# A mixture-of-experts stage whose expert weights are loaded from DRAM for each tile, with all tile rows loaded beforehand

## The chip, the core and the metric

The kernel runs on one core of one Trainium2 chip. The metric is the device time of one execution in microseconds (us). The core has five engines that run side by side and wait for each other with semaphores: TensorE (PE in the profile, with its weight loads as PEld), VectorE (DVE), ScalarE (ACT), GpSimd (POOL) and SyncE (SP). SP computes nothing here: it waits on semaphores and issues DMAs. Each engine works through its own program in order.

## The reference

Two layers are computed over 2048 tokens of 128 features. The last part of the second layer is a mixture of experts (MoE) with top-1 routing: each token goes through one of 8 experts, each a small two-layer network with its own weights.

```
hn = layernorm(xn) * ln2_g + ln2_b          # 2048 x 128
e  = argmax(hn @ gate_w + gate_b)           # one of 8 experts for each token
y  = relu(hn @ w1[e] + b1[e]) @ w2[e] + b2[e]     # w1: 128x512, w2: 512x128, all float32
x  = x + y                                  # (and the residuals of the other parts)
```

Everything before this (a recurrent filter and a gated network, attention, two Mamba scans) is outside the change.

## The kernel before

The program is a row of stages with a barrier of all engines between them (`end_stage`, line 59). The MoE is the last pair of stages.

`moe_prep_stage` (from line 1325) normalises the tokens, computes the gate, picks the expert and sorts the tokens by expert: each expert's tokens fill whole tiles of 128 rows, so there are at most NSLOT = 16 + 8 - 1 = 23 tiles. `S.eid` holds the expert of each tile, `S.pos` the row that each token goes to. The rows are scattered to DRAM (`S.x_dram`) by 16 indirect DMAs on POOL (line 1392), after a DMA on SP has filled `S.x_dram` with zeros (line 1372). In the same stage SP loads the weights of all 8 experts into one SBUF tensor `S.wall`: w1 as one DMA (line 1365), b1 (line 1366), b2 copied to all 128 partitions (line 1367) and w2 in eight DMAs (line 1369). SP waits for them at its end (line 1375).

`moe_stage` (from line 1486) runs over the 23 tiles, software-pipelined by hand. For tile s:

- SP: `load(s)` (line 1516) waits until tile s-3 is through (`y_psum`) and loads the 128 rows, 64 KB, into one of three buffers `x`; then `store(s-2)` (line 1522) waits for the result of tile s-2 and stores it to `S.y_dram`. The two alternate, so load(s+1) is queued behind store(s-2).
- DVE: reads the tile's expert number from `S.eid` into a register (line 1574) and copies that expert's 1156 columns of `S.wall` into one of three buffers `cur` (line 1577).
- PE: in its round s it transposes the rows of tile s+1 (line 1589, waits for the load), multiplies tile s by w1 in 4 matmuls that the profile shows as 8 records (line 1611), and then does the second layer of tile s-1: b2 through a matmul with a row of ones (line 1594, 2 records) and w2 (line 1597, 8 records).
- ACT: scales the transposed rows (line 1548), relu with bias b1 in four pieces (line 1565), copies the result out of PSUM into one of two buffers `y` (line 1555); before that copy it waits until the buffer's last store has landed (line 1554).

When all 23 stores have landed, POOL gathers the rows back to token order with 16 indirect DMAs (line 1539), DVE adds them to the residual (line 1581), and SP writes the output (line 1653).

Of the kernel before, what the change touches and what calls it, by code (L numbers as in the profile page):

```python
# [12 lines left out]
F32 = mybir.dt.float32  # L13
# [4 lines left out]
ACT = mybir.ActivationFunctionType  # L18
AX = mybir.AxisListType

P = 128
# [11 lines left out]
NE, NF = 8, 512  # L33
NFB = NF // P
NSLOT = NT + NE - 1
W2_AT = NF + NFB
B2_AT = W2_AT + NF
WROW = B2_AT + P
DI, NS, KC, DR = 256, 16, 4, 8
NB = DI // P  # L40

# [1281 lines left out]
def moe_prep_stage(nc, S, dr):  # L1323
# [4 lines left out]
    with ExitStack() as ctx:  # L1328
# [3 lines left out]
        def sem(n):  # L1332
            return S.enter_sem(nc, f"xp_{n}")
# [16 lines left out]
        w_load, dve_c, act_c, pool_c = sem("w_load"), sem("dve_chain"), sem("act_chain"), sem("pool_chain")  # L1350
        var_ready, rstd_ready, xn_ready, xn_psum, hn_ready = sem("var"), sem("rstd"), sem("xn_r"), sem("xn_psum"), sem("hn_r")
        lg_psum, oh_ready, counts = sem("lg_psum"), sem("oh_r"), sem("counts")
        all_in = sem("all_in")
        zeros_ready, zeroed, pos_ready, scattered = sem("zeros_r"), sem("zeroed"), sem("pos_r"), sem("scattered")
        block = ctx.enter_context(nc.Block())
        NCONST = 7
# [4 lines left out]
        @block.sync  # L1361
        def _(sp):
            sp.dma_start(gw[:, :], dr["gate_w"]).then_inc(w_load, 16)
            sp.dma_start(gb[:, :], dr["gate_b"]).then_inc(w_load, 16)
            sp.dma_start(S.wall[:, :, 0:NF], dr["w1"].rearrange("e h f -> h e f")).then_inc(all_in, 16)
            sp.dma_start(S.wall[:, :, NF:W2_AT], dr["b1"].rearrange("e p b -> p e b")).then_inc(all_in, 16)
            sp.dma_start(S.wall[:, :, B2_AT:WROW], dr["b2"].unsqueeze(0).to_broadcast([P, NE, P])).then_inc(all_in, 16)
            for e in range(NE):
                sp.dma_start(S.wall[:, e, W2_AT:B2_AT].rearrange("p (b h) -> p b h", h=P),
                             dr["w2"][e].rearrange("(b p) h -> p b h", p=P)).then_inc(all_in, 16)  # L1370
            sp.wait_ge(zeros_ready, 1)
            sp.dma_start(S.x_dram.rearrange("(s p) d -> p s d", p=P),
                         zeros[:, :].unsqueeze(1).to_broadcast([P, NSLOT, P])).then_inc(zeroed, 16)
            sp.wait_ge(w_load, 32)
            sp.wait_ge(all_in, 16 * (3 + NE))

        @block.gpsimd
        def _(pool):
# [107 lines left out]
def moe_stage(nc, S, dr):  # L1486

    with ExitStack() as ctx:  # L1488
        def sb(n, shape, dt=F32):
            return ctx.enter_context(nc.sbuf_tensor(f"xe_{n}", shape, dt))  # L1490

        def sem(n):
            return S.enter_sem(nc, f"xe_{n}")

        W = 3
        cur = sb("cur", [P, W, WROW])
        x, xT = sb("x", [P, W, P]), sb("xT", [P, 2, P])
        mid, y = sb("mid", [P, 2, NFB, P]), sb("y", [P, 2, P])
        ones = sb("ones", [1, P])
        picked = sem("picked")  # L1500
        moved = sb("moved", [P, NT, P])
        t_bank, m_bank, y_bank = S.banks[0:2], S.banks[2:4], S.banks[4:6]
        loaded = [sem(f"loaded{w}") for w in range(W)]
        stored = [sem("stored0"), sem("stored1")]
        gathered = [sem(f"gathered{c}") for c in range(NCH)]
        turned, xT_ready, mid_psum, mid_ready, y_psum, y_ready = (sem("turned"), sem("xT_r"), sem("mid_psum"), sem("mid_r"),
                                                                  sem("y_psum"), sem("y_r"))
# [6 lines left out]
        @block.sync  # L1514
        def _(sp):
            def load(s):
                w = s % W
                if s >= W:
                    sp.wait_ge(y_psum, s - W + 1)
                sp.dma_start(x[:, w, :], S.x_dram[P * s:P * (s + 1), :]).then_inc(loaded[w], 16)  # L1520

            def store(s):
                sp.wait_ge(y_ready, s + 1)
                sp.dma_start(S.y_dram[P * s:P * (s + 1), :], y[:, s % 2, :]).then_inc(stored[s % 2], 16)  # L1524

            for s in range(NSLOT):
                load(s)
                if s >= 2:
                    store(s - 2)
            store(NSLOT - 2)  # L1530
            store(NSLOT - 1)

        @block.gpsimd
        def _(pool):
            pool.memset(ones[:, :], 1.0).then_inc(ones_ready, 1)
            pool.wait_ge(stored[0], 16 * ((NSLOT + 1) // 2))
            pool.wait_ge(stored[1], 16 * (NSLOT // 2))
            for i in range(NT):
                pool.indirect_dma_start(moved[:, i, :], None, S.y_dram,  # L1539
                                        bass.IndirectOffsetOnAxis(ap=S.pos[:, i:i + 1], axis=0)).then_inc(gathered[i // TPC], 16)  # L1540

        @block.scalar
        def _(act):
            def turn(s):
                act.wait_ge(turned, s + 1)
                if s >= 2:
                    act.wait_ge(mid_psum, s - 1)
                act.activation(xT[:, s % 2, :], t_bank[s % 2][:, 0:P], ACT.Identity, bias=V("ln2_b"),  # L1548
                               scale=V("ln2_g")).then_inc(xT_ready, 1)

            def out(s):
                act.wait_ge(y_psum, s + 1)
                if s >= 2:
                    act.wait_ge(stored[s % 2], 16 * (s // 2))
                act.activation(y[:, s % 2, :], y_bank[s % 2][:, 0:P], ACT.Copy).then_inc(y_ready, 1)  # L1555

            turn(0)
            for s in range(NSLOT):
                if s + 1 < NSLOT:
                    turn(s + 1)  # L1560
                act.wait_ge(mid_psum, s + 1)
                if s >= 2:
                    act.wait_ge(y_psum, s - 1)
                for f in range(NFB):
                    act.activation(mid[:, s % 2, f, :], m_bank[s % 2][:, P * f:P * (f + 1)], ACT.Relu,
                                   bias=cur[:, s % W, NF + f:NF + f + 1]).then_inc(mid_ready, 1)
                if s >= 1:
                    out(s - 1)
            out(NSLOT - 1)

        @block.vector
        def _(dve):
            for s in range(NSLOT):
                e = dve.value_load(S.eid[0:1, s:s + 1], min_val=0, max_val=NE - 1)
                if s >= W:
                    dve.wait_ge(y_psum, s - W + 1)
                dve.tensor_copy(cur[:, s % W, :].unsqueeze(1), S.wall[:, bass.ds(e, 1), :]).then_inc(picked, 1)  # L1577
            for c in range(NCH):
                dve.wait_ge(gathered[c], 16 * TPC)
                r = S.res[:, TPC * c:TPC * (c + 1), :]  # L1580
                dve.tensor_tensor(r, r, moved[:, TPC * c:TPC * (c + 1), :], ALU.add).then_inc(added, 1)  # L1581

        @block.tensor
        def _(pe):
            def turn(s):
                pe.wait_ge(loaded[s % W], 16 * (s // W + 1))
                if s >= 2:
                    pe.wait_ge(xT_ready, s - 1)
                pe.transpose(t_bank[s % 2][:, 0:P], x[:, s % W, :], S.ident[:, :]).then_inc(turned, 1)  # L1589

            def output(s):
                if s >= 2:
                    pe.wait_ge(y_ready, s - 1)
                pe.matmul(y_bank[s % 2][:, 0:P], ones[:, :], cur[0:1, s % W, B2_AT:WROW], start=True, stop=False)  # L1594
                for f in range(NFB):
                    pe.wait_ge(mid_ready, NFB * s + f + 1)
                    mm = pe.matmul(y_bank[s % 2][:, 0:P], mid[:, s % 2, f, :], cur[:, s % W, W2_AT + P * f:W2_AT + P * (f + 1)],  # L1597
                                   start=False, stop=(f == NFB - 1))
                mm.then_inc(y_psum, 1)

            pe.wait_ge(ones_ready, 1)
            turn(0)
            for s in range(NSLOT):
                if s + 1 < NSLOT:
                    turn(s + 1)
                pe.wait_ge(xT_ready, s + 1)
                if s >= 2:
                    pe.wait_ge(mid_ready, NFB * (s - 1))
                pe.wait_ge(picked, s + 1)
                for f in range(NFB):  # L1610
                    mm = pe.matmul(m_bank[s % 2][:, P * f:P * (f + 1)], cur[:, s % W, P * f:P * (f + 1)], xT[:, s % 2, :],  # L1611
                                   start=True, stop=True)
                mm.then_inc(mid_psum, 1)
                if s >= 1:
                    output(s - 1)
            output(NSLOT - 1)


def moe(nc, S, dr):
    with ExitStack() as ctx:  # L1620
        S.pos = ctx.enter_context(nc.sbuf_tensor("x_pos", [P, NT], U32))
        S.eid = ctx.enter_context(nc.sbuf_tensor("x_eid", [P, NSLOT], I32))
        S.wall = ctx.enter_context(nc.sbuf_tensor("x_wall", [P, NE, WROW], F32))
        S.x_dram, S.y_dram = (nc.dram_tensor(f"x_{n}", [NSLOT * P, P], F32).ap() for n in ("rows", "done"))
        moe_prep_stage(nc, S, dr)
        S.end_stage(nc)
        moe_stage(nc, S, dr)
        S.end_stage(nc)
# [82 lines left out]
```

## Time and profile before

| | us |
|---|---|
| median of 3 runs | 1839.95 (1839.89 to 1840.34) |
| the profiled execution | 1845.69 |
| its span, first to last instruction | 1844.0 |
| MoE stage until its last result is in SBUF | 1646.79 to 1813.93 |
| gather, residual and output after it | 1813.95 to 1844.0 |

| engine | busy us of the span | share |
|---|---|---|
| PE | 1148.8 | 62% |
| DVE | 1260.3 | 68% |
| ACT | 845.7 | 46% |
| POOL | 508.4 | 28% |

The busy shares are means over stages with different limits; the stages before 1595 us are bound by other engines than the MoE stage is. For a change in one stage, the views to read are those of that stage: who waits for whom, the chain of work that ended last, and the timeline in order of time. A time of an instruction that begins with L is its line in the code; SPq and DVEq are the sequencers of SP and DVE, which issue DMAs and work on registers, and are not counted as busy. PEclk is the granted TensorE clock as a share of full speed: 0.50 is 1.2 GHz, 1.00 is 2.4 GHz.

### The profile page before, as it was taken

Reading aid. Unit: us, or ns where it says so; the run is one execution under the profiler, and the core shown is the slowest. Engines: PE = TensorE matmul, PEld = TensorE weight load, DVE = VectorE, ACT = ScalarE, POOL = GpSimd, SP = SyncE. Lnnn points to the kernel's source line nnn. Section 1 sums busy time; section 2 is a strip of 40 time slices with the busy share of each in tenths; the row PEclk is TensorE's granted clock in tenths of the full one; section 3 lists DMA queues with packets and bytes.
Section 4 is the critical chain, followed back from the end, with each engine's and each line's share of the span. In section 5 each row is a group of like instructions: output and inputs, shape, how many; then the busy total and the mean of one; then the engine's idle time right before and its main releaser. Section 6 shows DMA issues by size and latency. Waiting matters only on the chain. (4 is left out here: it accounts for less than half of the span.)

```text
span 1844.0 us, 17746 instructions
## 1 busy us (share of the span) xinstructions
PE 1148.8 (62%) x5865; PEld 398.3 (22%) x5865; DVE 1260.3 (68%) x1893; ACT 845.7 (46%) x1217; POOL 508.4 (28%) x473
## 2 busy tenths in 40 slices
PE   0341499999999999999873133337513333526662
PEld 0130022222222222222330000004200000425552
DVE  8943899999999999996111599991139999410000
ACT  2220067777777777777625244431524444202220
POOL 1201000000000000000002699980249999130003
PEclk9765599999999999999986555557855555655555
DMA  0012010001001100000003666600176552310001
GB/s 28 0 62 83 24 58 1 1 22 46 10 1 38 39 1 1 1 2 1 3 19 119 125 127 137 137 1 22 63 171 138 124 108 43 110 59 18 17 18 53
DMA packets 64682, 93.51 MB, mean 51 GB/s; under 512 B 8998, under 2 KB 29750, under 8 KB 64590
## 3 DMA queue, kind: packets, MB, share of 16 engines
q1 hardware_dynamic: 63566, 90.27, 19.8%
q0 software_dynamic: 1024, 2.10, 0.4%
q8 instruction: 47, 0.77, 0.2%
q14 instruction: 45, 0.37, 0.1%
HBM read 74.88 MB, written 17.17 MB: 50 GB/s over the span
## 5 line engine op out<-in xcount | busy, mean ns | idle before, releaser
L658 DVE TENSOR_REDUCE at_mpart<-psum 128x1 f32<-128x512 f32 x1024 | 656.5, 685 | 49.3 <-PE psum L719 30.0
L637 ACT ACTIVATE at_probs<-psum 128x1024 f32<-128x1024 f32 x512 | 496.2, 1021 | 272.8 <-PE psum L748 272.6
L761 PE MATMUL psum<-at_probs,at_vg 128*32 128x512 f32 x2048 | 273.6, 606 | 0.4 <-ACT at_probs L637 0.4
L748 PE MATMUL psum<-at_qs,at_ks 75*128 75x512 bf16 x1024 | 269.3, 384 | 1.3 <-ACT at_probs L637 0.2
L719 PE MATMUL psum<-at_ks,at_qs 64*128 64x512 bf16 x512 | 207.9, 406 | 84.9 <-DMA at_km<-k_parts 50.6
L723 PE MATMUL psum<-at_km,at_qm 64*128 64x512 bf16 x512 | 207.9, 406 | 0.0
L613 POOL CAST at_m<-at_mneg 128x16 bf16<-128x16 f32 x16 | 3.1, 197 | 698.2 <-DVE at_mneg L663 698.2
L1225 POOL TENSOR_TENSOR msf_inject<-msf_dus,msf_bs 128x512 f32<-128x512 f32 x128 | 159.7, 1299 | 28.5 <-DMA msf_cs<-m_bc 28.5
L1225 POOL TENSOR_TENSOR msb_inject<-msb_dus,msb_bs 128x512 f32<-128x512 f32 x128 | 158.4, 1265 | 27.0 <-DMA msb_cs<-m_bc 27.0
L1244 PE MATMUL psum<-msf_hc,m_stack 128*32 128x512 f32 x256 | 61.0, 1042 | 161.6 <-DVE msf_hc L1169 152.6
L1244 PE MATMUL psum<-msb_hc,m_stack 128*32 128x512 f32 x256 | 60.1, 1027 | 160.9 <-DVE msb_hc L1169 151.9
L719 PEld LDWEIGHTS psum<-at_ks,at_qs 64*128 64x128 bf16 x512 | 47.7, 93 | 385.0 <-DVE at_mpart L658 331.1
L1577 DVE COPY xe_cur<-x_wall 128x1156 f32 x23 | 17.5, 763 | 159.0 <-PE psum L1597 134.4
L1153 ACT ACTIVATE psum<-msf_dts,m_aneg 128x512 f32<-128x512 f32 x128 | 85.5, 686 | 48.6 <-DVE msf_hp L1196 19.4
L748 PEld LDWEIGHTS psum<-at_qs,at_ks 75*128 75x128 bf16 x1024 | 78.2, 98 | 135.3 <-issue 52.0
L1153 ACT ACTIVATE psum<-msb_dts,m_aneg 128x512 f32<-128x512 f32 x128 | 85.5, 686 | 47.1 <-DVE msb_hp L1196 19.2
L1196 DVE TENSOR_TENSOR_SCAN psum<-psum,msb_last,msb_inject 128x512 f32<-128x512 f32 x66 | 82.5, 1273 | 0.0
L1196 DVE TENSOR_TENSOR_SCAN psum<-psum,msf_last,msf_inject 128x512 f32<-128x512 f32 x66 | 82.5, 1273 | 0.0
L1539 POOL DMA_INDIRECT xe_moved<-x_done,x_pos x16 | 15.7, 981 | 173.3 <-DMA x_done<-xe_y 168.7
L1589 PE MATMUL psum<-ident,xe_x 128*128 128x128 f32 x23 | 10.8, 472 | 83.4 <-DMA xe_x<-x_rows 83.4
L1239 PE MATMUL psum<-m_u,m_diag 128*32 128x512 f32 x128 | 30.3, 1028 | 49.5 <-PEq L62 49.5
L1169 DVE TENSOR_TENSOR msf_hc<-psum,msf_cs 128x512 f32<-128x512 f32 x88 | 58.6, 667 | 0.0
(273 smaller groups left out, 1421.3 us busy)
## 6 DMA issues: line engine op xcount, KB each, us to landing
msf_dts<-m_dt SPq DMA_DIRECT2D x32, 256.0 KB
msf_dus<-m_dtu SPq DMA_DIRECT2D x32, 256.0 KB
msb_dts<-m_dt SPq DMA_DIRECT2D x32, 256.0 KB
msb_dus<-m_dtu SPq DMA_DIRECT2D x32, 256.0 KB
at_qs<-q_parts SPq DMA_DIRECT2D x48, 96.0 KB
at_ks<-k_parts SPq DMA_DIRECT2D x48, 96.0 KB
msf_bs<-m_bc SPq DMA_DIRECT2D x16, 256.0 KB
msf_cs<-m_bc SPq DMA_DIRECT2D x16, 256.0 KB
```

What stands on the lines that cost most here:

```text
L637: act.activation(probs[:, u % 2, p, :], s_pair[p], ACT.Exp, scale=float(HD) ** -0.5).then_inc(probs_ready, 1)
L658: dve.reduce_max(mpart[:, s % 2, 2 * jp + b, i, kc:kc + 1], ring[x % 3], AX.X).then_inc(ring_free, 1)
L719: pe.matmul(ring[x % 3], S.qs[0:HALF, buf, q], S.ks[0:HALF, buf, k], start=True, stop=True)\
L723: pe.matmul(ring[y % 3], S.qm[64:64 + HALF, buf, q], S.km[64:64 + HALF, buf, k], start=True, stop=True)\
L748: mm = pe.matmul(s_banks[p][b], S.ks[0:DM, g % 2, j * T + kt * P:j * T + (kt + 1) * P], S.qs[0:DM, g % 2, j * T + c * CH:j * T + (c + 1) * ...
L761: mm = pe.matmul(o_bank[VW * j:VW * (j + 1), :], vg[:, g % 2, kt, j, :], probs[:, u % 2, j // 2, CH * (j % 2):CH * (j % 2 + 1)], start=(kt ...
L1153: act.activation(decay[k % ND], dts[:, i % 2, j, :], ACT.Exp, scale=S.aneg[:, n:n + 1]).then_inc(decay_ready, 1)
L1169: dve.tensor_tensor(hc[:, r % 2, j, :], hv[by_dve[k] % NH2], cs[:, c % 2, q, :], ALU.mult).then_inc(dve_weighed, 1)
L1196: dve.tensor_tensor_scan(h, decay[k % ND], inject[:, k % NI, :], before if c else 0.0, ALU.mult, ALU.add).then_inc(scanned, 1)
L1225: pool.tensor_tensor(inject[:, k % NI, :], dus[:, i % 2, j, :], bs[:, c % 2, q, :], ALU.mult).then_inc(injected, 1)
L1239: pe.matmul(y_bank[i % 2][GC * j:GC * (j + 1), :], S.diag[:, b, GC * j:GC * (j + 1)], S.u[:, b, cols(c)], start=True, stop=False, tile_pos ...
L1244: mm = pe.matmul(y_bank[i % 2][GC * j:GC * (j + 1), :], S.stack[:, :], hc[:, r % 2, j, :], start=False, stop=(q == NQ - 1), tile_position= ...
```

## The change

`S.wall` is gone, with its eleven loads in the prep stage and the wait for them. In the MoE stage DVE no longer reads expert numbers or copies weights. SP does both: `load(s)` reads the expert number of tile s into a register of SP and issues four DMAs from DRAM at an address that depends on it (w1 256 KB, b1 2 KB, w2 256 KB, b2 0.5 KB), into one of five buffers. The rows of all 23 tiles are loaded by four DMAs at the start of the stage (`rows(n)`, six tiles each), the first ahead of load(0), the others behind it. Results have a buffer for each of the 23 tiles, so ACT's wait for a store's landing is gone. store(s-5) stands behind load(s) on SP.

```diff
-            sp.dma_start(S.wall[:, :, 0:NF], dr["w1"].rearrange("e h f -> h e f")).then_inc(all_in, 16)
-            sp.dma_start(S.wall[:, :, NF:W2_AT], dr["b1"].rearrange("e p b -> p e b")).then_inc(all_in, 16)
-            sp.dma_start(S.wall[:, :, B2_AT:WROW], dr["b2"].unsqueeze(0).to_broadcast([P, NE, P])).then_inc(all_in, 16)
-            for e in range(NE):
-                sp.dma_start(S.wall[:, e, W2_AT:B2_AT].rearrange("p (b h) -> p b h", h=P),
-                             dr["w2"][e].rearrange("(b p) h -> p b h", p=P)).then_inc(all_in, 16)
...
-            sp.wait_ge(all_in, 16 * (3 + NE))
...
-        W = 3
+        W = 5
+        NX = 4
+        XT = -(-NSLOT // NX)
...
                 if s >= W:
                     sp.wait_ge(y_psum, s - W + 1)
-                sp.dma_start(x[:, w, :], S.x_dram[P * s:P * (s + 1), :]).then_inc(loaded[w], 16)
+                e = sp.value_load(S.eid[0:1, s:s + 1], min_val=0, max_val=NE - 1)
+                sp.dma_start(w1[:, w, :], dr["w1"][bass.ds(e, 1)].rearrange("o h f -> h (o f)")).then_inc(loaded[w], 16)
+                sp.dma_start(b1[:, w, :], dr["b1"][bass.ds(e, 1)].rearrange("o p b -> p (o b)")).then_inc(loaded[w], 16)
+                sp.dma_start(w2[:, w, :, :], dr["w2"][bass.ds(e, 1)].rearrange("o (b p) h -> p (o b) h", p=P))\
+                    .then_inc(loaded[w], 16)
+                sp.dma_start(b2[:, w, :], dr["b2"][bass.ds(e, 1)]).then_inc(loaded[w], 16)
 
             def store(s):
                 sp.wait_ge(y_ready, s + 1)
-                sp.dma_start(S.y_dram[P * s:P * (s + 1), :], y[:, s % 2, :]).then_inc(stored[s % 2], 16)
-
-            for s in range(NSLOT):
+                sp.dma_start(S.y_dram[P * s:P * (s + 1), :], y[:, s, :]).then_inc(stored, 16)
+
+            def rows(n):
+                part = slice(XT * n, min(XT * (n + 1), NSLOT))
+                sp.dma_start(x[:, part, :], S.x_dram.rearrange("(s p) d -> p s d", p=P)[:, part, :]).then_inc(x_in[n], 16)
+
+            rows(0)
+            load(0)
+            for n in range(1, NX):
+                rows(n)
+            for s in range(1, NSLOT):
                 load(s)
-                if s >= 2:
-                    store(s - 2)
-            store(NSLOT - 2)
-            store(NSLOT - 1)
+                if s >= W:
+                    store(s - W)
+            for s in range(NSLOT - W, NSLOT):
+                store(s)
...
-                if s >= 2:
-                    act.wait_ge(stored[s % 2], 16 * (s // 2))
-                act.activation(y[:, s % 2, :], y_bank[s % 2][:, 0:P], ACT.Copy).then_inc(y_ready, 1)
+                act.activation(y[:, s, :], y_bank[s % 2][:, 0:P], ACT.Copy).then_inc(y_ready, 1)
...
-            for s in range(NSLOT):
-                e = dve.value_load(S.eid[0:1, s:s + 1], min_val=0, max_val=NE - 1)
-                if s >= W:
-                    dve.wait_ge(y_psum, s - W + 1)
-                dve.tensor_copy(cur[:, s % W, :].unsqueeze(1), S.wall[:, bass.ds(e, 1), :]).then_inc(picked, 1)
...
-                pe.wait_ge(loaded[s % W], 16 * (s // W + 1))
+                pe.wait_ge(x_in[s // XT], 16)
...
-                pe.wait_ge(picked, s + 1)
+                pe.wait_ge(loaded[s % W], 16 * 4 * (s // W + 1))
```

## Rows read from the trace of the kernel before

**Rows 1.** Chain of work that ended last, one tile: start, us, what
```profile
1723.52 0.32 SPq L1524
1723.89 1.88 DMA xe_x<-x_rows
1725.81 0.48 PE psum L1589
1726.29 1.71 PE psum L1611 x8
1727.99 0.72 PE psum L1594 x2
1728.71 2.02 PE psum L1597 x8
1730.75 0.29 ACT xe_y L1555
```

**Rows 2.** Waits, 1646 to 1815 us: who waited for whom, total us, times, longest
```profile
PE psum L1589 <- DMA xe_x<-x_rows: 83.4, 21, 30.3
```

**Rows 3.** Timeline of PE at the stage's end: start, us, line, count [idle before]
```profile
1801.54 0.48 PE L1589 MATMUL psum<-ident,xe_x 128*128 128x128 f32 x1 [2.69 <-DMA xe_x<-x_rows]
1801.81 1.92 PE L1611 MATMUL psum<-xe_xT,xe_cur 128*128 128x128 f32 x8
1803.65 0.79 PE L1594 MATMUL psum<-xe_cur,xe_ones 1*128 1x128 f32 x2
1804.38 2.08 PE L1597 MATMUL psum<-xe_cur,xe_mid 128*128 128x128 f32 x8
1806.24 1.92 PE L1611 MATMUL psum<-xe_xT,xe_cur 128*128 128x128 f32 x8
```

**Rows 4.** Timeline, first result of the stage on PE
```profile
1653.58 0.48 PE L1594 MATMUL psum<-xe_cur,xe_ones 1*128 1x128 f32 x2
1654.00 1.16 PE L1597 MATMUL psum<-xe_cur,xe_mid 128*128 128x128 f32 x8
```

**Rows 5.** Stretches: from:to, length, busy us (count) of PE, PEld, DVE, ACT, POOL, PEclk, DMA share, GB/s
```profile
1524.00:1529.00 5.00, 3.64 (x16) 0.68 (x16) 5.00 (x7) 3.19 (x6) 5.00 (x5) 0.50 1.07 211
1554.00:1555.00 1.00, 0.08 (x4) 0.00 (x0) 1.00 (x3) 0.52 (x1) 1.00 (x2) 0.85 0.00 0
1592.00:1595.00 3.00, 1.72 (x5) 0.41 (x3) 2.63 (x13) 0.00 (x0) 0.00 (x0) 1.00 0.00 0
1656.00:1658.00 2.00, 0.27 (x2) 0.28 (x2) 0.06 (x1) 0.00 (x0) 0.00 (x0) 0.67 0.23 66
1806.20:1813.60 7.40, 7.40 (x30) 6.22 (x28) 0.00 (x0) 1.70 (x6) 0.00 (x0) 0.50 0.06 18
```

**Rows 6.** DVE's sequencer, reading an expert number (ns min/median/max)
```profile
L1574 DVEq TENSOR_LOAD <-x_eid x23: 298/300/556, 1646.8 to 1791.5; - x23
L1574 DVEq FUSED_REGOPS  x23: 190/190/213, 1647.4 to 1791.8; - x23
L1577 DVEq FUSED_REGOPS  x23: 57/57/65, 1647.7 to 1798.9; - x23
```

**Rows 7.** Timeline of SP: DMA issues, start, us in all, count
```profile
1.24 2.07 SPq L135 DMA_DIRECT2D l_x<-in_x  x4
1596.21 0.43 SPq L1365 DMA_DIRECT2D x_wall<-in_w  x1
1601.59 8.27 SPq L1369 DMA_DIRECT2D x_wall<-in_w  x8
```

**Rows 8.** Timeline of the prep stage: what the scatter's first DMA waited for
```profile
1623.08 1.20 POOL L1392 DMA_INDIRECT x_rows<-xp_xn,x_pos  x1 [26.57 <-DVE x_pos L1459]
```

**Rows 9.** Timeline: last copy of a result, before the gather
```profile
1813.65 0.28 ACT L1555 ACTIVATE xe_y<-psum 128x128 f32<-128x128 f32 x1 [2.45 <-PE psum L1597]
```

**Rows 10.** Timeline of PE in the Mamba stage, second of two equal stretches
```profile
1550.44 1.94 PE L1244 MATMUL psum<-msb_hc,m_stack 128*32 128x512 f32 x8 [4.57 <-DVE msb_hc L1169]
1552.12 1.96 PE L1239 MATMUL psum<-m_u,m_diag 128*32 128x512 f32 x8
```

More of the change, by code:

```diff
@@ L35 @@
 NSLOT = NT + NE - 1
-W2_AT = NF + NFB
-B2_AT = W2_AT + NF
-WROW = B2_AT + P
 DI, NS, KC, DR = 256, 16, 4, 8
@@ L1352, in moe_prep_stage @@
         lg_psum, oh_ready, counts = sem("lg_psum"), sem("oh_r"), sem("counts")
-        all_in = sem("all_in")
         zeros_ready, zeroed, pos_ready, scattered = sem("zeros_r"), sem("zeroed"), sem("pos_r"), sem("scattered")
@@ L1493, in sem @@
             return S.enter_sem(nc, f"xe_{n}")
-        W = 3
-        cur = sb("cur", [P, W, WROW])
-        x, xT = sb("x", [P, W, P]), sb("xT", [P, 2, P])
-        mid, y = sb("mid", [P, 2, NFB, P]), sb("y", [P, 2, P])
+        W = 5
+        NX = 4
+        XT = -(-NSLOT // NX)
+        w1, w2, b1, b2 = sb("w1", [P, W, NF]), sb("w2", [P, W, NFB, P]), sb("b1", [P, W, NFB]), sb("b2", [1, W, P])
+        x, xT = sb("x", [P, NSLOT, P]), sb("xT", [P, 2, P])
+        mid, y = sb("mid", [P, 2, NFB, P]), sb("y", [P, NSLOT, P])
         ones = sb("ones", [1, P])
-        picked = sem("picked")
         moved = sb("moved", [P, NT, P])
@@ L1503, in moe_stage @@
         loaded = [sem(f"loaded{w}") for w in range(W)]
-        stored = [sem("stored0"), sem("stored1")]
+        x_in = [sem(f"x_in{n}") for n in range(NX)]
+        stored = sem("stored")
         gathered = [sem(f"gathered{c}") for c in range(NCH)]
@@ L1535, in _ @@
             pool.memset(ones[:, :], 1.0).then_inc(ones_ready, 1)
-            pool.wait_ge(stored[0], 16 * ((NSLOT + 1) // 2))
-            pool.wait_ge(stored[1], 16 * (NSLOT // 2))
+            pool.wait_ge(stored, 16 * NSLOT)
             for i in range(NT):
@@ L1565, in _ @@
                     act.activation(mid[:, s % 2, f, :], m_bank[s % 2][:, P * f:P * (f + 1)], ACT.Relu,
-                                   bias=cur[:, s % W, NF + f:NF + f + 1]).then_inc(mid_ready, 1)
+                                   bias=b1[:, s % W, f:f + 1]).then_inc(mid_ready, 1)
                 if s >= 1:
@@ L1585, in turn @@
             def turn(s):
-                pe.wait_ge(loaded[s % W], 16 * (s // W + 1))
+                pe.wait_ge(x_in[s // XT], 16)
                 if s >= 2:
                     pe.wait_ge(xT_ready, s - 1)
-                pe.transpose(t_bank[s % 2][:, 0:P], x[:, s % W, :], S.ident[:, :]).then_inc(turned, 1)
+                pe.transpose(t_bank[s % 2][:, 0:P], x[:, s, :], S.ident[:, :]).then_inc(turned, 1)
             def output(s):
@@ L1593, in output @@
                     pe.wait_ge(y_ready, s - 1)
-                pe.matmul(y_bank[s % 2][:, 0:P], ones[:, :], cur[0:1, s % W, B2_AT:WROW], start=True, stop=False)
+                pe.matmul(y_bank[s % 2][:, 0:P], ones[:, :], b2[:, s % W, :], start=True, stop=False)
                 for f in range(NFB):
                     pe.wait_ge(mid_ready, NFB * s + f + 1)
-                    mm = pe.matmul(y_bank[s % 2][:, 0:P], mid[:, s % 2, f, :], cur[:, s % W, W2_AT + P * f:W2_AT + P * (f + 1)],
+                    mm = pe.matmul(y_bank[s % 2][:, 0:P], mid[:, s % 2, f, :], w2[:, s % W, f, :],
                                    start=False, stop=(f == NFB - 1))
@@ L1608, in _ @@
                     pe.wait_ge(mid_ready, NFB * (s - 1))
-                pe.wait_ge(picked, s + 1)
+                pe.wait_ge(loaded[s % W], 16 * 4 * (s // W + 1))
                 for f in range(NFB):
-                    mm = pe.matmul(m_bank[s % 2][:, P * f:P * (f + 1)], cur[:, s % W, P * f:P * (f + 1)], xT[:, s % 2, :],
+                    mm = pe.matmul(m_bank[s % 2][:, P * f:P * (f + 1)], w1[:, s % W, P * f:P * (f + 1)], xT[:, s % 2, :],
                                    start=True, stop=True)
@@ L1622, in moe @@
         S.eid = ctx.enter_context(nc.sbuf_tensor("x_eid", [P, NSLOT], I32))
-        S.wall = ctx.enter_context(nc.sbuf_tensor("x_wall", [P, NE, WROW], F32))
         S.x_dram, S.y_dram = (nc.dram_tensor(f"x_{n}", [NSLOT * P, P], F32).ap() for n in ("rows", "done"))
```

## The prediction

> **What bounds the kernel now.** Only the MoE stage changes in its rhythm, so the page's shares of the whole span say little; I read the stage's own views. First the chain that ended last. One tile takes 7.52 us in it: SP issues a store (0.32), then the load of the rows takes 1.88 from issue to landing, then PE works 0.48 + 1.71 + 0.72 + 2.02 = 4.93, then ACT copies the result (0.29) and SP can issue the next store [rows 1]. The reader is to see that a DMA stands in the chain of each tile, although three buffers exist: the load of tile s+1 is queued on SP behind store(s-2), which waits for ACT's copy. The list of waits says the same: PE waited 83.4 us in 21 waits for rows, 30.3 of them from before the stage [rows 2], so about 53 us, 2.6 for each of 20 tiles. Then the timeline of the last tiles, where all rows are in: PE goes from line 1589 at 1801.54 to the next line 1611 at 1806.24 without a wait for rows, 4.70 us [rows 3]. That is what PE needs for a tile at 1.2 GHz. Last the clock: it is 0.50 nearly throughout, but the first result was computed at the higher level, with line 1597 in 1.16 us where it takes 2.02 later [rows 1, 4].
>
> **What is removed from the chain.** The row load (1.88), the copy (0.29), the store's issue (0.32) and the gaps between them leave the chain: 7.52 - 4.70 = 2.82 us per tile. The rows come beforehand, and nothing on PE waits for SP's stores. What is next is one of three: PE at 1.2 GHz (4.70), PE at 2.4 GHz, or SP, which now issues five DMAs per tile instead of two.
>
> **PE at 2.4 GHz.** Line 1594 takes 0.42 until line 1597 starts (1654.00 - 1653.58) [rows 4]; line 1597 until the next group 1806.24 - 1804.38 = 1.86 at 1.2 GHz [rows 3], of which 8 records of 128 float32 columns stream half as long at the double clock; 1.16 with its end [rows 4], so 1.0 until the next can start. Line 1611 likewise 1803.65 - 1801.81 = 1.84 becomes 0.99, the transpose 0.27 becomes 0.11. Sum 2.5 us.
>
> **SP per tile.** The trace has no read of an expert number on SP, but DVE makes the same one: 0.298 for the load, 0.190 for register operations, and with its check and gaps 0.59 [rows 6]. Each of the four DMAs has an address from the register; the nearest row is DVE's 0.057 for its dynamic copy [rows 6], with a gap some 0.11, four times 0.43. Upper end: the 0.190 kind each time, with its gap 0.24, 0.96 in all. The issues: w1 0.43 as line 1365; w2 is the pattern of layer 0's input (128 partitions, four pieces of 512 B), 2.07 / 4 = 0.52; b1 and b2 not over 0.43 each [rows 7]. With gaps of 0.05: 0.59 + 0.43 + 0.43 + 0.52 + 0.86 + 0.20 = 3.03 us for a load; with the store's 0.32 + 0.05 [rows 1] 3.40. Bounds: 2.9 if the small ones and the address work cost less, 4.0 with the upper price of addresses. The w2 loads in the prep stage were issued every 8.27 / 8 = 1.03 us [rows 7], twice 0.52: there SP was held up by full queues, 256 KB each 1.03 us being 254 GB/s. A tile here moves 516 KB in and 64 KB out; at that rate 2.3 us, under the 3.40 of the issues, so the transfers hide behind the issuing and no queue stays full except at the start.
>
> The Trainium skill ("DMA: Bandwidth & Descriptors", Latency and other measured facts) gives a floor of some 600 ns for a tensor load. The trace differs, 0.298 here [rows 6], and decides; by the page's figure each tile would cost SP 0.3 us more, by an estimate 23 x 0.3 = 7 us on the total.
>
> **The clock.** Which of the two levels PE gets decides between 4.70 and SP's 3.40. What rows show: at the stage's start PE did line 1611 twice with a transpose between, from 1649.88 on without idle time, and at 1653.6 it ran at 2.4 GHz [rows 4]; it fell back after the first wait for rows, 1655.2 to 1657.7 [rows 5]. In the last 7.4 us of the stage PE was also without a long gap and stayed at 0.50 [rows 5]. There each stretch of full matmuls between two of line 1594 was 1.86 + 1.84 = 3.7 us. In Mamba, stretches of 3.6 us, eight records of line 1244 and eight of line 1239, come several times: the one from 1524.4 left the clock at 0.50, the equal one from 1550.4 raised it [rows 5, 10]. So stretches of this length raise it sometimes. After the change the stretch is w2, transpose, w1: 1.86 + 0.27 + 1.84 = 4.0 us, longer than all of these, and it comes each tile. I expect a rise within the first few tiles in which PE runs without waiting. Does it stay? At SP's pace PE idles 3.40 - 2.5 = 0.9 us per tile in small pieces; from 1592 to 1595 PE was busy for 1.72 of 3.0 us and the clock stayed at 1.00 [rows 5], and the fall in this stage came with 2.5 us idle in one piece. If it falls, PE lags, has no waits again, and rises again. I take 2.4 GHz for most of the stage.
>
> The skill ("TensorE: Matmul & The Clock Gate", Loop structure matters more than you think) says that matmuls back to back, with the DMAs overlapped, keep the clock up, and that a wait on a DMA before each matmul group lets it fall. The last 7.4 us, back to back and at 0.50 [rows 5], do not bear that out fully, which is why the slow clock keeps a chance below.
>
> **The other edits.** In prep the loads leave SP, not the path: the scatter waited for DVE's positions until 1623.08 [rows 8], with the zero fill long issued; the stage's SP wait ended before that. I cost this at nothing (bounds -1 and +0.5, should the DMA traffic have held up anything). DVE's copies (0.76 each) were beside PE; ACT's wait for a landed store did not end last. ACT per tile is about 1.9 us at either clock, under 3.40. The end, the last store and the gather, is the same.
>
> **The sum**, from the stage's start. Before, the last copy ended at 1813.93 [rows 9], 167.1 us after 1646.79. After: rows(0) 0.6, load(0) 3.0, the other three row DMAs 1.7; 2 MB are then asked for by 5.3 us and take about 8 us at 254 GB/s, which holds SP up by 1: 6.3. Loads 1 to 4: 4 x 3.03 = 12.1, to 18.4. Loads 5 to 22 with a store each: 18 x 3.40 - 0.37 = 60.8, to 79.2. The last lands some 1.7 later (rows land 1.88 from issue [rows 1]), 80.9; then w1 0.99, second layers of tiles 21 and 22 with 1.4 and 1.6, and ACT 0.3: 85.2. The gain is 167.1 - 85.2 = 82 us. Against the profiled execution 1845.69 becomes 1764 (its span 1762); it lies 5.7 above the median of the runs, all of it outside what changes, so the median goes from 1839.95 to 1758.
>
> **Rivals.** *The clock stays at 1.2 GHz* and PE is the bound: tile 1 can start at 11 us (load 1 issued by 9.3), its w1 and the layer before it take 4.5, then 21 x 4.70 = 98.7 and 2.8 for the end: 117. Gain 50, time 1790. For it: the rows of the last 7.4 us. Against it: the longer stretch. *SP's address work is dear* or the clock is up only in part: SP at 4.0 to 4.7 per tile adds 22 x 0.6 to 22 x 1.2, 13 to 27 us: 1771 to 1785. *Slower than before:* SP is the bound with an issue price for a DMA at a register's address that no row shows. From 167 - 15 = 152 us over 22 loads, 6.9 us per tile, it loses: that is 0.9 more for each of the four DMAs, three times the price of an issue. At 7.5 it would be 1853. Against it: every DMA of SP is already made by the same hardware queue at run time. *That it does nothing* needs PE to wait as before; since the rows no longer hang on results, only a clock and an SP both bad could do it.
>
> **How the numbers follow.** 0.61 for SP-bound at the high clock, 1747 to 1771, forecast 1758; 0.17 for 1771 to 1786; 0.17 for the slow clock, 1786 to 1796; 0.03 for SP between 5 and 6.9 us per tile; 0.02 for slower. The low end is SP at 2.9: 22 x 0.5 = 11 less. The range 1747 to 1792 leaves out about 0.15. What a measurement of this kernel can tell from no change is about 0.2%: faster 0.97, same 0.01, slower 0.02.
>
> **What would show it.** In the changed kernel's timeline SP issues without waits from load 1 on, a new one each 3.4 us with the five DMAs; PE's waits are for w1 or w2, some 0.9 us a tile; PEclk is near 1.00 from the third tile or so; line 1597 is near 1.16. I am wrong if PEclk stays 0.50 with PE without idle time (1790), if a dynamic issue is far over 0.5 us, or if PE waits on ACT at the high clock.

## The result, and the profile after

The changed kernel takes 1754.57 us in the median (1753.94 to 1760.18, 4 runs), beside 1839.92 for the kernel before (1835.68 to 1840.34, 4 runs). The ratio is 0.955, with an interval of 0.952 to 0.957: 85 us less. The profiled execution took 1753.94, its span 1752.0.

| | before | after |
|---|---|---|
| prep stage, first DMA issue | 1595.33 | 1586.34 |
| MoE stage begins | 1646.79 | 1637.82 |
| MoE stage until its last result is copied | 167.1 | 84.7 |
| from there to the end of the span | 30.0 | 29.5 |

Two things stand in this table. The stage lost 82.5 us. And it began 9.0 us earlier, all of which had been gained before the prep stage began, in stages whose code is the same. The stage begins between 1637 and 1647 us in all the kernels below, and not in the order of what they change. So differences between kernels are read from the stage's own length below, and the total only where it was taken in several runs.

SP in the changed kernel, one tile from its timeline (start, us, line):

```profile
1666.30 0.34 SPq L1512 DMA_DIRECT2D xe_w<-in_w  x1
1666.82 0.33 SPq L1513 DMA_DIRECT2D xe_b<-in_b  x1
1667.25 0.38 SPq L1514 DMA_DIRECT2D xe_w<-in_w  x1
1667.82 0.28 SPq L1516 DMA_DIRECT2D xe_b<-in_b  x1
1668.15 0.34 SPq L1520 DMA_DIRECT2D x_done<-xe_y  x1
1669.44 0.34 SPq L1512 DMA_DIRECT2D xe_w<-in_w  x1
```

Lines 1512 to 1516 are w1, b1, w2 and b2, line 1520 is a store of a result. From one w1 to the next it is 3.14 us, and nothing in between is a wait. The 0.95 us between the end of the store's issue at 1668.49 and the next w1 is the read of the expert number and the address. The instructions there, by line, with ns min/median/max:

```profile
L1511 SPq TENSOR_LOAD <-x_eid x23: 447/457/505, 1638.2 to 1711.5; - x23
L1511 SPq FUSED_REGOPS  x23: 152/152/187, 1638.8 to 1712.0; - x23
L1512 SPq FUSED_REGOPS  x23: 42/42/48, 1639.1 to 1712.2; - x23
L1512 SPq MOVE xe_w<-in_w x23: 29/29/43, 1639.2 to 1712.3; - x23
```

PE in the changed kernel, in its timeline where the clock rises:

```profile
1658.27 0.42 PE L1585 MATMUL psum<-ident,xe_x 128*128 128x128 f32 x1
1658.49 1.92 PE L1607 MATMUL psum<-xe_xT,xe_w 128*128 128x128 f32 x8
1660.33 0.78 PE L1590 MATMUL psum<-xe_b,xe_ones 1*128 1x128 f32 x2
1661.04 1.16 PE L1593 MATMUL psum<-xe_w,xe_mid 128*128 128x128 f32 x8
1662.03 0.27 PE L1585 MATMUL psum<-ident,xe_x 128*128 128x128 f32 x1
1662.14 1.06 PE L1607 MATMUL psum<-xe_xT,xe_w 128*128 128x128 f32 x8
```

Line 1585 is the transpose, 1607 is w1, 1590 the product of ones and b2, 1593 is w2. They answer to [rows 3 and 4]. w1 and w2 take 1.06 and 1.16 us where they took 1.92 and 2.08. The stretches of the changed kernel (length, busy us and count of PE, PEld, DVE, ACT, POOL, PEclk, DMA share, GB/s):

```profile
1637.80:1722.50 84.70, 70.02 (x437) 60.88 (x437) 0.00 (x0) 40.97 (x138) 0.19 (x1) 0.82 0.64 179
1656.00:1661.00 5.00, 5.00 (x21) 4.38 (x20) 0.00 (x0) 2.17 (x9) 0.00 (x0) 0.50 0.60 168
1661.00:1702.00 41.00, 37.68 (x275) 32.80 (x275) 0.00 (x0) 25.41 (x87) 0.00 (x0) 1.00 0.67 184
1702.00:1705.00 3.00, 0.34 (x4) 0.11 (x3) 0.00 (x0) 0.63 (x2) 0.00 (x0) 1.00 0.54 151
1705.00:1712.00 7.00, 6.98 (x29) 6.18 (x29) 0.00 (x0) 2.35 (x9) 0.00 (x0) 0.52 0.57 170
```

PEclk is 0.50 while the first loads arrive, 1.00 from 1661.0, and 0.50 again from about 1705 until 1712. What came before the fall is in the same trace. SP's timeline, then PE's, then the DMA queues from 1700 to 1703 us (packets, MB, share of the 16 engines' time):

```profile
1698.66 0.34 SPq L1512 DMA_DIRECT2D xe_w<-in_w  x1
...
1700.18 0.28 SPq L1516 DMA_DIRECT2D xe_b<-in_b  x1
...
1702.33 1.12 SPq L1513 DMA_DIRECT2D xe_b<-in_b  x1
...
1705.02 1.76 PE L1607 MATMUL psum<-xe_xT,xe_w 128*128 128x128 f32 x8 [2.68 <-DMA xe_b<-in_b]
...
q8 instruction: 1, 0.02, 3.9%
```

PE had nothing for 2.68 us, and the clock fell. Counted back from the last tile on both engines, the w1 product at 1705.02 is that of tile 18, and tile 18's loads are those issued from 1698.66 to 1700.46, on time and each at its usual length. Of the landings that the trace has for this tile's semaphore all but the last came by 1702.73, and the last at 1704.88. The issue on SP that took 1.12 us instead of 0.33 belongs to tile 19 and can't have held up tile 18. Both the late piece and the long issue overlap in time with one packet of 16 KB on q8, the queue that the profile names instruction: it took 1.87 us from 1701.20 (the 3.9% above). That this packet held them up is likely and not shown. The kernel before fell to the low level in its wait of 2.57 us [rows 5] too, but the size of one wait doesn't tell alone: in the kernel with rows per tile below, the clock fell at 1688.7 after waits of 1.09 and 1.49 us, and in the unbroken control it stayed up through one of 1.69.

PE's waits for weights are few and add up to 10.3 us, 5.0 of them for the first two tiles (the list of waits, the stage only):

```profile
PE psum L1607 <- DMA xe_b<-in_b: 10.3, 8, 2.8
```

against 83.4 for rows in the kernel before, 30.3 of them from before the stage [rows 2]. Once PE has caught up with the loads, from 1680 on, it waits for one now and then, 0.3 to 0.7 us, at the full clock, and SP waits once between two loads, for 0.3 us: that points to SP as the bound, which the experiments test.

### The profile page after: what moved, and what is told of

Same layout as the page of the kernel before. It is cut to its first block and busy times, and to the rows that moved or that the text cites. A ratio compares the mean times of both kernels' runs of the same rounds, so it can differ in the third digit from the quotient of the medians.

```text
span 1752.0 us, 17902 instructions
## 1 busy us (share of the span) xinstructions
PE 1101.0 (63%) x5865; PEld 358.7 (20%) x5865; DVE 1242.1 (71%) x1870; ACT 843.4 (48%) x1217; POOL 510.1 (29%) x473
## 5 line engine op out<-in xcount | busy, mean ns | idle before, releaser
L716 PE MATMUL psum<-at_ks,at_qs 64*128 64x512 bf16 x512 | 208.0, 406 | 85.2 <-DMA at_km<-k_parts 50.7
L1193 DVE TENSOR_TENSOR_SCAN psum<-psum,msf_last,msf_inject 128x512 f32<-128x512 f32 x66 | 82.5, 1274 | 0.0
L1193 DVE TENSOR_TENSOR_SCAN psum<-psum,msb_last,msb_inject 128x512 f32<-128x512 f32 x66 | 82.5, 1273 | 0.0
L1166 DVE TENSOR_TENSOR msb_hc<-psum,msb_cs 128x512 f32<-128x512 f32 x88 | 58.6, 667 | 0.0
L1139 ACT ACTIVATE msb_last<-psum 128x1 f32<-128x1 f32 x66 | 11.3, 171 | 88.8 <-DVE msb_hc L1166 88.8
```

Of the source, the lines that this page charges most:

```text
L716: pe.matmul(ring[x % 3], S.qs[0:HALF, buf, q], S.ks[0:HALF, buf, k], start=True, stop=True)\
L1166: dve.tensor_tensor(hc[:, r % 2, j, :], hv[by_dve[k] % NH2], cs[:, c % 2, q, :], ALU.mult).then_inc(dve_weighed, 1)
L1193: dve.tensor_tensor_scan(h, decay[k % ND], inject[:, k % NI, :], before if c else 0.0, ALU.mult, ALU.add).then_inc(scanned, 1)
```

## The experiments

All stage lengths are from the stage's first instruction to the copy of its last result, in the profiled execution of each kernel. The clock is the mean PEclk of the stage. A kernel for which no range of totals is given was executed once.

| kernel | stage us | clock in it | us per tile in steady state |
|---|---|---|---|
| before | 167.1 | 0.51 | 7.52 |
| changed | 84.7 | 0.82 | 2.50 to 3.8, one 7.28 |
| rows only, weights from SBUF | 66.7 | 0.90 | 2.50 |
| load ahead of the store | 62.5 | 0.95 | 2.50 |
| changed, fixed address | 70.4 | 0.88 | 2.50 |
| changed, half the bytes | 82.5 | 0.86 | 2.50 to 3.4, one 4.39 |
| changed, rows per tile | 93.7 | 0.80 | 2.50 to 5.8 |
| changed, three buffers | 117.3 | 0.64 | 3.2 to 6.3 |
| changed, broken stretch | 138.9 | 0.50 | 5.67 |
| changed, unbroken control | 84.8 | 0.88 | 2.73 to 4.7 |
| rows only, bias on DVE | 51.2 | 0.91 | 1.90 |
| load ahead of the store, bias on DVE | 48.8 | 0.94 | 1.90 |

**Rows only.** Is it the weights from DRAM, or the rows beforehand, that helped?

```diff
-                sp.dma_start(x[:, w, :], S.x_dram[P * s:P * (s + 1), :]).then_inc(loaded[w], 16)
...
+            for n in range(NX):
+                part = slice(XT * n, min(XT * (n + 1), NSLOT))
+                sp.dma_start(x[:, part, :], S.x_dram.rearrange("(s p) d -> p s d", p=P)[:, part, :]).then_inc(x_in[n], 16)
+            for s in range(NSLOT):
+                sp.wait_ge(y_ready, s + 1)
+                sp.dma_start(S.y_dram[P * s:P * (s + 1), :], y[:, s, :]).then_inc(stored, 16)
```

> One part of the change alone: the rows of all tiles are loaded beforehand and all results keep a buffer, as in the changed kernel, but the weights stay as before (eight experts in SBUF, DVE copies the tile's expert). Theory: the rhythm of the changed kernel is set by SP's issuing (3.15 us a tile in its trace), and the gain comes from rows that no longer wait for results; then without SP's work TensorE is the bound at its 2.5 us a tile, the clock rises after the first tiles, and the stage takes 62 to 67 us until its last copy, against 84.7 in the changed kernel: 1732 to 1738 in all. Rival 1, loading the weights from DRAM is what helped: then this kernel is slower than the changed one, at 1775 to 1790 (TensorE at 1.2 GHz, 4.65 us a tile, or DVE's copies in the way). Rival 2, TensorE and not SP bounds the changed kernel: then both are within 5 us.

Measured: stage 66.7 us, 1742.1 in all (1739.5 to 1745.9, 4 runs; ratio to the kernel before 0.950, 0.947 to 0.952). The total is some 4 us over the upper end of the expectation, the stage within it; this kernel's stage began at 1644.0, 6 us later than the changed kernel's. Its stretches:

```profile
1644.00:1710.70 66.70, 62.17 (x437) 55.85 (x437) 17.53 (x23) 40.86 (x138) 0.19 (x1) 0.90 0.16 45
1660.00:1700.00 40.00, 40.00 (x305) 36.14 (x305) 12.21 (x16) 28.32 (x96) 0.00 (x0) 1.00 0.10 27
```

PE is busy for 40.00 of 40.00 us at the full clock: it is the bound, at 2.50 us a tile. The weights from DRAM did not help; they cost the stage 84.7 - 66.7 = 18 us. All the gain is in the rows and results.

**Load ahead of the store.** Does it take all rows beforehand, or only another order on SP?

```diff
                 load(s)
-                if s >= 2:
-                    store(s - 2)
-            store(NSLOT - 2)
-            store(NSLOT - 1)
+                if s >= XW:
+                    store(s - XW)
+            for s in range(NSLOT - XW, NSLOT):
+                store(s)
```

(on the kernel before, with XW = 5 buffers for rows and for results instead of 3 and 2)

> The kernel before with nothing but a deeper row queue: five buffers for the rows and five for the results, the rows still loaded tile by tile, and store(s-5) instead of store(s-2) behind load(s); weights as before. Theory (the row load stood behind a store that waits for a result two tiles back, and that order alone cost the 2.8 us a tile and the clock): the same as the kernel with all rows loaded beforehand, stage 65 to 69 us, total about 1740. Rival (it takes all rows in SBUF beforehand, because a row load in the loop still lands late): 75 us or more.

Measured: stage 62.5 us, below the expectation; 1734.0 in all (1732.6 to 1736.1, 4 runs; ratio 0.943, 0.940 to 0.946). Every interval between results was 2.50 us from the first on, but for the last two (2.39 and 1.50), behind which no more tile comes. It is 4 us shorter than with all rows beforehand: the clock was up by 1648.0, 6.4 us after the stage's start, where the kernel with all rows beforehand had it 13.2 us after (1657.2). Half of the 4 us is that the first rows come sooner: PE's first instruction is 1.9 us after the stage's start here and 3.9 us there. The rest is the clock, which rose 4.5 us after PE's first instruction and not 9.3; why it did so is not shown. So five buffers and an order in which no load stands behind a late store are all that the stage needed.

**Fixed address.** What do reading the expert number and the address in a register cost? This kernel leaves out the routing: tile s takes the weights of expert s modulo 8.

```diff
-                e = sp.value_load(S.eid[0:1, s:s + 1], min_val=0, max_val=NE - 1)
+                e = s % NE
...
-                sp.dma_start(w1[:, w, :], dr["w1"][bass.ds(e, 1)].rearrange("o h f -> h (o f)")).then_inc(loaded[w], 16)
+                sp.dma_start(w1[:, w, :], dr["w1"][e:e + 1].rearrange("o h f -> h (o f)")).then_inc(loaded[w], 16)
```

> The changed kernel with the expert number of each tile a constant (tile number modulo 8), so that SP neither reads it nor works out addresses; the same bytes are moved, but the wrong experts' weights are applied, so the output is not the reference's. It measures the price of the register address. Theory (SP's issuing is the bound): 0.46 + 0.15 + 0.02 for the read and its check, 0.04 + 0.03 for each address, and their gaps leave SP, 3.15 becomes about 2.0 us a tile, TensorE's 2.5 binds, and the stage takes 68 to 75 us instead of 84.7. Rival (the DMA engines bound it, 0.67 of their time taken in the changed kernel at 184 GB/s): no change, 82 to 87 us.

Measured: 70.4 us, as the theory said, with as many bytes. The loads that waited for nothing followed each other every 1.73 us, where the changed kernel needs 2.80. The experts also come in another order than in the changed kernel. In the middle of the stage:

```profile
1660.00:1700.00 40.00, 40.00 (x306) 36.13 (x305) 0.00 (x0) 28.36 (x97) 0.00 (x0) 1.00 0.83 232
```

PE is the bound again, and the DMA engines carried 232 GB/s at a share of 0.83, against 184 at 0.67 in the changed kernel. The transfers were not what limited that kernel. They aren't far from it either.

**Half the bytes.** The same question from the other side: from the sixth tile on half of w1 and w2 is left out.

```diff
+                nf, nb = (NF, NFB) if s < W else (NF // 2, NFB // 2)
-                sp.dma_start(w1[:, w, :], dr["w1"][bass.ds(e, 1)].rearrange("o h f -> h (o f)")).then_inc(loaded[w], 16)
+                sp.dma_start(w1[:, w, 0:nf], dr["w1"][bass.ds(e, 1), :, 0:nf].rearrange("o h f -> h (o f)")).then_inc(loaded[w], 16)
```

> The changed kernel with w1 and w2 of every tile from the sixth on loaded only by half (256 of 512 columns, two of four blocks), the same number of DMAs; the other half of each buffer keeps what an earlier tile left there, so the output is not the reference's. Theory (SP's issuing): the stage stays at 83 to 86 us, DMA share falls from 0.67 to about 0.4. Rival (the transfers bound it): 18 tiles of half the bytes save up to 1 us each or more, 65 to 75 us. A small gain of 1 to 3 us would say that full queues hold SP up now and then (the three issues of about 1 us in the changed kernel's trace).

Measured: 82.5 us, 2.1 less than the changed kernel, just outside the theory's 83 to 86:

```profile
1641.20:1723.80 82.60, 67.87 (x437) 58.34 (x437) 0.00 (x0) 41.03 (x138) 0.20 (x1) 0.86 0.45 127
1665.00:1705.00 40.00, 37.70 (x275) 32.62 (x274) 0.00 (x0) 25.41 (x87) 0.00 (x0) 1.00 0.36 100
```

DMA share fell to 0.36, and PE was busy for 37.70 of 40 us, against 37.68 of 41 in the changed kernel. The 2 us are not SP's: it ended its last load 76.7 us after the stage's start, beside 76.4 in the changed kernel. They are PE's at the end, which began its last w1 1.4 us after that load and not 3.9, since in this execution the clock did not fall again. So half the bytes gave SP nothing, and an issue of 1.57 us instead of 0.38 occurred here too:

```profile
L1515 SPq DMA_DIRECT2D xe_w<-in_w x23: 383/383/1572, 1643.7 to 1717.1; - x23
```

**Rows per tile.** The rows part undone, the weights part kept.

```diff
                 sp.dma_start(b2[:, w, :], dr["b2"][bass.ds(e, 1)]).then_inc(loaded[w], 16)
+                sp.dma_start(x[:, w, :], S.x_dram[P * s:P * (s + 1), :]).then_inc(x_in[w], 16)
...
-            rows(0)
             load(0)
-            for n in range(1, NX):
-                rows(n)
```

> The changed kernel with one part undone: the rows of tile s are loaded in load(s), behind its weights, into five buffers, instead of beforehand. Theory (SP's issuing is the bound): each tile costs SP 0.43 + 0.05 more, 3.15 becomes 3.6 us, and the stage grows by 17 x 0.45 = 8 us less 2 for the shorter start: 88 to 94 us, if the clock stays up as long. Rival (the transfers or TensorE bound it): 82 to 86 us.

Measured: 93.7 us, 9.0 more, and SP's period grew from 3.14 to 3.62 us:

```profile
1671.15 0.35 SPq L1512 DMA_DIRECT2D xe_w<-in_w  x1
1671.68 0.34 SPq L1513 DMA_DIRECT2D xe_b<-in_b  x1
1672.12 0.38 SPq L1514 DMA_DIRECT2D xe_w<-in_w  x1
1672.69 0.28 SPq L1516 DMA_DIRECT2D xe_b<-in_b  x1
1673.02 0.34 SPq L1517 DMA_DIRECT2D xe_x<-x_rows  x1
1673.42 0.42 SPq L1521 DMA_DIRECT2D x_done<-xe_y  x1
1674.77 0.35 SPq L1512 DMA_DIRECT2D xe_w<-in_w  x1
```

One issue more per tile, some 0.48 us more per tile: SP sets the pace. Between these two executions the rows beforehand are worth 9 us, and 17 tiles by 0.48 account for 8 of them. The clock fell twice here and once in the changed kernel.

**Three buffers.**

```diff
-        W = 5
+        W = 3
```

> The changed kernel with three weight buffers instead of five (and store(s-3) behind load(s)). Load(s) may then start only when the second layer of tile s-3 is done. Theory: from there the issues take 2.8 and the landing 1.7 us, 4.5 to 4.9 in all, for which TensorE has only one tile's work, so it idles about 2.4 us in every two tiles; at 2.4 GHz a tile would take 3.7 us, and when the clock falls 4.7; stage 95 to 115 us. Rival (five buffers do nothing since SP is behind anyway): 83 to 88 us.

Measured: 117.3 us, 2 over the upper end of the theory; the rival is out. The clock was up for only 33 of the 117 us (mean 0.64), so the size that I had wrong was the share of the slow clock: with 13 waits of PE for loads, 16.9 us in all, and 4.65 us a tile at the low level, less is left of the gain.

**Broken stretch, and its control.** What raises the clock?

```diff
                 pe.wait_ge(loaded[s % W], 16 * 4 * (s // W + 1))
+                pe.matmul(S.banks[6][:, 0:P], ones[:, :], b2[:, s % W, :], start=True, stop=True)
```

> The changed kernel with one more product of the row of ones and b2 in each tile, into an unused part of PSUM, between the transpose and w1; the result isn't used. It breaks the stretch w2, transpose, w1 in two, as the last tiles of the kernel before had it broken, and costs TensorE 0.42 us at 2.4 GHz and 0.72 at 1.2. Theory (an unbroken stretch of full matmuls raises the clock): PEclk stays at 0.50 in nearly all of the stage, 5.4 us a tile, 125 to 135 us. Rival (TensorE at work without idle time is enough): it rises as before, 2.9 us a tile stay under SP's 3.15, and the stage takes 84 to 88 us.

The control has the same product at another place:

```diff
+                pe.matmul(S.banks[6][:, 0:P], ones[:, :], b2[:, s % W, :], start=True, stop=True)
                 pe.matmul(y_bank[s % 2][:, 0:P], ones[:, :], b2[:, s % W, :], start=True, stop=False)
```

> The control of the kernel with the broken stretch: the same extra product of ones and b2 in each tile, but directly ahead of the one that is there, so that w2, transpose and w1 still follow each other without it. Theory (the place matters, an unbroken stretch raises the clock): PEclk rises after some tiles as in the changed kernel, 2.7 to 2.9 us a tile stay under SP's 3.15, stage 84 to 92 us. Rival (the place doesn't matter, only that the extra product takes time from full matmuls): PEclk stays at 0.50 and the stage takes 135 to 140 us, as with the broken stretch (138.9).

Measured: 138.9 us with the stretch broken and 84.8 with the control. The stage of the first, then of the control:

```profile
1644.50:1783.50 139.00, 130.65 (x483) 107.33 (x483) 0.00 (x0) 41.72 (x138) 0.20 (x1) 0.50 0.39 109
```

```profile
1642.70:1727.50 84.80, 70.14 (x483) 61.60 (x483) 0.00 (x0) 40.96 (x138) 0.19 (x1) 0.88 0.65 179
```

PE did the same instructions in both (483 records). In the first it was busy 130.65 of 139 us, with no wait for loads after the start, and the clock never left 0.50. The place of one product, two records in each tile, decides 54 us. That the broken tile took 5.67 and not 5.4 us is part of the 138.9 being over the expected 135: from the transpose to the next product it was 0.35 us there, where it is 0.21 to w1 in the changed kernel at the same level, and w1 took 2.01 until the next start and not 1.84. The next kernels show the same from the other side.

**The bias on DVE.** On the kernel with rows only, DVE adds b2 while it copies the result out of PSUM; the product with ones and ACT's copy go.

```diff
+            def out(s):
+                dve.wait_ge(y_psum, s + 1)
+                dve.tensor_tensor(y[:, s, :], y_bank[s % 2][:, 0:P], cur[:, s % W, B2_AT:WROW], ALU.add).then_inc(y_ready, 1)
...
-                pe.matmul(y_bank[s % 2][:, 0:P], ones[:, :], cur[0:1, s % W, B2_AT:WROW], start=True, stop=False)
```

> The kernel with only the rows loaded beforehand (weights from SBUF), with b2 added by DVE while it copies the result out of PSUM, in place of the product of ones and b2 on TensorE and of ACT's copy. Theory (TensorE's 2.5 us bounds that kernel, 0.42 of it for the product): 2.1 us a tile, and at the start the clock rises no later; stage 66.7 - 21 x 0.42 = 57 to 59 us, total 8 to 10 under that kernel. Rival (ACT at 1.6 us with its waits, or DVE with 0.76 for the weights and 0.3 for the result, becomes the bound): 2.3 us a tile or more, 62 us and up.

Measured: 1.90 us a tile, stage 51.2, total 1722.5 (1719.9 to 1726.4, 4 runs; ratio 0.938, 0.935 to 0.941). I had expected 2.1 and 57 to 59. The total is 19.6 us under the kernel with rows only, 15.5 of them from the stage. The product cost 0.60 us of PE's 2.50, not 0.42: it also lengthened its neighbours. In this kernel the pair of w1 and w2 needs 0.90 and 0.89 from start to start, against 0.99 each around the product.

**Order and bias together.** Both of these on the kernel before.

```diff
+                if s >= XW:
+                    store(s - XW)
...
-                pe.matmul(y_bank[s % 2][:, 0:P], ones[:, :], cur[0:1, s % W, B2_AT:WROW], start=True, stop=False)
...
+                dve.tensor_tensor(y[:, s % XW, :], y_bank[s % 2][:, 0:P], cur[:, s % W, B2_AT:WROW], ALU.add).then_inc(y_ready, 1)
```

> Both edits that helped most, on the kernel before: rows tile by tile with five buffers for rows and results and store(s-5) behind load(s), and b2 added by DVE in place of the product with ones and of ACT's copy. Weights from SBUF. Theory: 1.9 us a tile, as the kernel with the bias on DVE showed, and the early start of the kernel with the deeper row queue: stage 62.5 - 21 x 0.6 = 50 us (48 to 52), total 1721 to 1724, no more than 10 below the kernel with the bias on DVE. Rival (at 1.9 us a tile the row loads and stores on SP or their landing become late): stage above 54.

Measured: stage 48.8 us, as expected; total 1725.4 (1723.4 to 1728.0, 5 runs; ratio 0.937, 0.935 to 0.939), 1.4 over the upper end. The total is not under that of the bias on DVE alone, whose ratio was 0.938: the two can't be told apart by total, since the stage began at 1647.2 in the one profile and at 1637.1 in the other. Either is about 30 us faster than the changed kernel by its total. PE in its timeline, without a gap:

```profile
1672.05 1.06 PE L1618 MATMUL psum<-xe_xT,xe_cur 128*128 128x128 f32 x8
1672.94 1.06 PE L1604 MATMUL psum<-xe_cur,xe_mid 128*128 128x128 f32 x8
1673.84 0.27 PE L1597 MATMUL psum<-ident,xe_x 128*128 128x128 f32 x1
1673.95 1.06 PE L1618 MATMUL psum<-xe_xT,xe_cur 128*128 128x128 f32 x8
```

## Why the prediction was right, step by step

The forecast was 1758, the median 1754.6. The stage was forecast at 85.2 us and took 84.7.

- *The row load, the copy and the store's issue leave the chain, and PE at 1.2 GHz needs 4.70.* Held: while the clock was low the changed kernel gave a result every 4.65 us. Shown by the kernels with rows only and with the load ahead of the store.
- *PE at 2.4 GHz needs 2.5.* Held to the digit, 2.50 in five kernels.
- *SP needs 3.40 for a tile with its store.* It was 3.14. The term has three parts. The read of the expert number was priced from DVE at 0.59 and is 0.76 on SP, from the end of the store's issue and its gap to the first address (0.46 for the load where DVE needs 0.30). The addresses and the gaps were 0.68 in all and are 0.71. The issues were 0.43, 0.43, 0.52 and 0.43 and are 0.34, 0.33, 0.38 and 0.28, 0.48 less in all. The rows that the forecast names for the issues hold none of b1 or b2. A DMA with a register's address, whose price no row of before showed, has an issue that is no dearer than with a fixed one (the four take 1.33 together, and 0.33, 0.43, 0.43 and 0.36 or 1.55 with fixed addresses), and some 0.1 for its address.
- *The transfers hide behind the issuing.* Shown: without the number's read and the register address 70.4, with half the bytes 82.5 and SP no sooner at its end. A tile's bytes are 514.5 KB in and not 516, which changes nothing.
- *The sum.* SP ended its last load at 76.4 us after the stage's start (b2 at 1713.90 and 0.28) where the sum had 79.2, although three issues took 1.36, 0.94 and 1.12 us. PE began the last w1 at 1718.11, 3.9 us after that and not 1.7: it was still catching up from the 7 us at 1.2 GHz after 1705. The 2.8 us too many on SP and the 2.2 too few on PE cancel. That the total of the stage came within 0.5 us is luck; SP as the bound and the levels of PE are not.
- *The clock rises within a few tiles and stays for most of the stage.* Held, 0.82 in the mean. The reason given, that it matters where the products with ones stand between the full ones, and that PE being without idle time is not enough, is now shown by the pair of kernels with the same instructions. When the clock rises isn't foretold by it: in the changed kernel PE was at work without idle time from 1649.06, and the clock rose at 1661.0. The statement of the Trainium skill that the prediction drew on ("TensorE: Matmul & The Clock Gate", Loop structure matters more than you think), that matmuls back to back keep the clock up, holds in the control. It does not help with the kernel with the broken stretch: there PE had no waits either and never got the full clock. Had it kept the clock up there too, an estimate from the control gives about 85 us, and 138.9 were measured. I had not foreseen a fall in the middle of the stage. It came with one late load. The prediction also has the clock fall back after the first wait for rows in the kernel before; it fell at 1656.69, in that wait.
- *The rivals.* None came true: PEclk was 0.82 in the mean and not 0.50, and SP took 3.14 a tile and not 4.0 or more. One sum among them is off: SP at 4.7 per tile is 1.3 over 3.40 and not 1.2, so 29 us and 1787 where 1785 stands.
- *The prep stage costs nothing, either way.* It lasted 1646.79 - 1595.33 = 51.5 us before and 1637.82 - 1586.34 = 51.5 after, the loads of eight experts' weights included and left out.
- *The total.* The profiled execution of before lay 5.7 above its median; I took that to lie outside what changes, and the start of the stage, 9.0 us earlier after, shows it did. But 85 us between the medians is 82.5 from the stage and the rest from stages that did not change. What varies in those from one execution or program to the next was not tried.

What stays open: why an issue on SP now and then takes about 1 us more. It happens with half the bytes (1.57), with fixed addresses (1.80), with three buffers (1.59) and in the kernel with rows per tile, there on stores (1.31 and 1.17); the slower pace of the last two does not prevent it. The traces narrow it down: of the 17 issues over 0.8 us that SP makes in the stages of all these kernels behind their first 9 us, 16 overlap in time with a packet of 16 KB on the instruction queue q8, which takes 0.9 to 1.9 us, and the other one with a packet of 8 KB on q14, also of the kind instruction. There are three or four such packets of 16 KB in the length of a stage, not each with a long issue beside it. That they hold SP up is argued from this coincidence; no kernel here changes them.

## What to carry to other kernels

When an engine waits for a load although buffers are free, look at what stands ahead of the load's issue on its queue: here a store that waited for a result two tiles back cost 2.8 us a tile and the clock, and five buffers for rows and for results with the load issued first gave back 105 of the stage's 167 us, with nothing else changed. A DMA per tile is an issue per tile: four with an address from a register and a store made SP the bound at 3.1 us, where the copy from SBUF was free beside TensorE. And a small product between full ones, such as a bias by a row of ones, is dear beyond its own length; an idle engine that copies the result anyway can add the bias.

## What the runs showed of the hardware

- Two kernels with the same 483 TensorE records in the stage ran at a mean clock of 0.50 and of 0.88 of full speed, for the place of one product of a single row: 138.9 and 84.8 us. In the slow one TensorE had no wait for loads in steady state.
- The product of ones and b2 (two records, one row) took 0.42 us until the next started, but its removal saved 0.60 us of 2.50, since w1 and w2 beside it went from 0.99 to 0.90 us each.
- Reading a number from SBUF into a register took 0.457 us on SP and 0.298 on DVE [rows 6]. The Trainium skill's floor of some 600 ns ("DMA: Bandwidth & Descriptors", Latency and other measured facts) is above both.
- The long issues on SP, 0.8 to 1.8 us instead of 0.3 to 0.5, coincide with single packets of 16 KB on the queue that the profile names instruction (in one of 17 cases 8 KB). In the changed kernel such a packet took 1.87 us from 1701.20, and the last piece of a load in flight landed 2.15 us after all others.
- The DMA engines moved 232 GB/s in pieces of 256 KB, 2 KB, 256 KB, 0.5 KB and 64 KB with TensorE at work without idle time beside them.
